# Sixteen words allocated in front of the weights of a directional convolution

## The reference

```python
x = x + _L0_conv_ref(_gn(x), L0_conv_dw_weight, L0_conv_pw_weight, L0_conv_pw_bias)
# in _L0_conv_ref:
h = gelu(depthwise3x3(x))                              # 256 channels
maps = einsum('bchw,oc->bohw', h, pw_weight) + pw_bias # 8 x 256 channels
for i, (dx, dy) in enumerate(OFFSETS8):
    diff = roll(x, (dy, dx)) - x
    out = out + maps[:, i] * diff
```

## Time and profile before

| | before |
|---|---|
| median of 3 runs | 2271.36 us |
| profiled execution | 2271.6 us |
| its span | 2269.8 us |
| granted TensorE clock, mean | 0.999 |
| TensorE busy | 97% |
| VectorE busy | 91% |
| GpSimd busy | 87% |
| ScalarE busy | 81% |

### The profile page before, as it was taken

The page is one execution under the profiler, slowest core; times in us unless marked ns, Lnnn a source line. Parts: engine busy times, 40 slices in busy tenths (PEclk is TensorE's granted clock), DMA queues, the critical chain, the costliest instruction groups (busy, mean ns, idle before and its releaser), DMA issues.

```text
span 2269.8 us, 28684 instructions
## 1 busy us (share of the span) xinstructions
PE 2209.1 (97%) x10752; PEld 2008.5 (88%) x10752; DVE 2056.1 (91%) x2234; ACT 1844.6 (81%) x2762; POOL 1981.4 (87%) x857
## 2 busy tenths in 40 slices
PE   1999999999999999999999999999999999999998
PEld 1999989999999999999989999999999999899997
DVE  7998989999999998998989999998999999999995
ACT  5978888788887978888788887888878888797774
POOL 5889898899888998899898988899888998889985
PEclk9999999999999999999999999999999999999999
DMA  6245263443725436164452644427353371542414
GB/s 179 51 82 116 49 115 88 90 98 56 156 41 106 95 54 153 33 108 95 77 127 39 116 98 84 103 49 136 68 98 90 64 156 33 106 98 49 98 33 73
DMA packets 47083, 202.13 MB, mean 89 GB/s; under 512 B 3040, under 2 KB 7136, under 8 KB 45664
## 3 DMA queue, kind: packets, MB, share of 16 engines
q0 software_dynamic: 30192, 94.97, 25.7%
q1 hardware_dynamic: 16752, 105.34, 18.0%
HBM read 104.88 MB, written 146.80 MB: 111 GB/s over the span
## 4 chain that ended last, share of the span: by engine, by line
PE 88%; DVE 5%; ACT 4%; issue 2%; DMA 0%; POOL 0%; SPq 0%; ACTq 0%; DVEq 0%
PE psum L913 88%; ACT psum L590 1%; DVE psum L705 1%; ACT hid L575 1%; DVE psum L785 1%; ACT psum L561 1%; DVE acc L727 1%; DVE products L705 1%; DVE psum L776 1%; DMA acc<-x 0%; ACT psum L565 0%; DVE acc L757 0%; POOL hlo L338 0%; DVE fields L808 0%; DVE part_sums L795 0%
## 5 line engine op out<-in xcount | busy, mean ns | idle before, releaser
L590 ACT ACTIVATE psum<-psum,bias,rstd 128x448 f32<-128x448 f32 x1792 | 1205.9, 694 | 384.6 <-PE psum L913 381.9
L369 POOL TENSOR_TENSOR acc<-acc,products 128x896 f32<-128x896 f32 x333 | 1167.1, 3505 | 240.2 <-DVE products L705 232.5
L913 PE MATMUL psum<-hhi,w_hi 128*128 128x448 f32 x3584 | 1321.7, 369 | 53.9 <-ACT hhi L580 45.5
L913 PE MATMUL psum<-hhi,w_lo 128*128 128x448 f32 x3584 | 1312.3, 366 | 0.0
L913 PE MATMUL psum<-hlo,w_hi 128*128 128x448 f32 x3584 | 1022.1, 366 | 0.3 <-POOL hlo L338 0.3
L785 DVE SCALAR_TENSOR_TENSOR psum<-xn,dw_f,psum 128x896 f32<-128x896 f32 x768 | 883.1, 1150 | 83.0 <-ACT psum L565 79.5
L913 PEld LDWEIGHTS psum<-hhi,w_hi 128*128 128x128 f32 x3584 | 672.6, 188 | 137.1 <-issue 45.5
L913 PEld LDWEIGHTS psum<-hlo,w_hi 128*128 128x128 f32 x3584 | 672.3, 188 | 59.7 <-POOL hlo L338 0.9
L913 PEld LDWEIGHTS psum<-hhi,w_lo 128*128 128x128 f32 x3584 | 672.8, 188 | 57.6
L705 DVE TENSOR_TENSOR products<-psum,fields 128x896 f32<-128x896 f32 x555 | 603.3, 1087 | 38.8 <-ACT psum L590 38.8
L705 DVE TENSOR_TENSOR acc<-psum,fields 128x896 f32<-128x896 f32 x224 | 242.6, 1090 | 53.2 <-ACT psum L590 51.8
(11 more groups left out here) (67 smaller groups left out, 449.0 us busy)
## 6 DMA issues: line engine op xcount, KB each, us to landing
out<-acc POOLq DMA_DIRECT2D x96, 896.0 KB, 7.7
out<-x SPq DMA_DIRECT2D x16, 3136.0 KB, 12.6
xpad<-x SPq DMA_DIRECT2D x30, 1568.0 KB, 15.1
out<-acc POOLq DMA_DIRECT2D x15, 448.0 KB, 5.6
acc<-x SPq DMA_DIRECT2D x4, 784.0 KB, 6.9
xpad<-pw_t SPq DMA_DIRECT2D x1, 2048.0 KB, 12.2
out<-products SPq DMA_DIRECT2D x2, 224.0 KB, 1.9
dw_f<-dw SPq DMA_DIRECT2D x1, 9.0 KB, 8.1
```

Source lines behind the costliest of these rows:

```text
L369: nc.gpsimd.tensor_tensor(a, a, p, ALU.add).then_inc(added_s, 1)
L590: nc.scalar.activation(m, m, ACT.Identity, bias=bias[ip][:, g, d:d + 1], scale=rstd[ip][:, g:g + 1]).then_inc(biased_s, 1)
L913: last = nc.tensor.matmul(maps(q)[:, side, :], w[:, kk, col:col + P], h_part(h, t, nl, kk), start=s == 0, stop=s == len(steps) - 1)
```

## The change

One tensor of sixteen float32 words a partition is allocated between `fields` and `w_hi`. Nothing reads or writes it.

```diff
@@ -111,6 +111,8 @@
         first = sums_t[:, 0:HALVES * H * W]
         first = first.rearrange("p (g c r w) -> p g c r w", g=HALVES, c=SLICES, w=W)
         w_raw = xpad_t[1][:, 0:HALVES * DIRS * C].rearrange("p (k m) -> p k m", k=HALVES)
+
+        sb("gap", [P, 16])
         w_hi = sb("w_hi", [P, HALVES, DIRS * C], F32R)
         w_lo = sb("w_lo", [P, HALVES, DIRS * C], F32R)
         dw_f = sb("dw_f", [P, HALVES, 9])
```

## The result

The changed kernel takes 2255.61 us in the median of six runs (2250.48 to 2258.2), against 2271.46 us before (2271.27 to 2272.06). The ratio is 0.9929, with a 95% interval of 0.9918 to 0.9939: 0.7% faster, where I had forecast no change. The scatter is new too: 7.7 us between the runs of one kernel, against 0.8 before.

What follows compares the result with a forecast made beforehand. PE was taken as the bound, by 10752 matmuls times their spacing. The sum 2269.8 + 0 + 0 + 0, and 1.8 outside, gave 2271.6 us profiled and 2271.4 for the median; range 2262 to 2281.

Steps and rivals of the forecast that it cites:

- The bound: On PE, time is nearly 10752 matmuls times their 203.75 ns spacing; each nanosecond of spacing is 10.75 us.
- What can tell the two starts apart: Weight starts at 32 and 96 of 128 bytes: only a structure of 128 bytes or more can distinguish them.
- The count of 128-byte blocks (five and five): A 512-byte weight read touches five 128-byte blocks from either start; the first gives 8 columns in place of 24.
- The load's cover: On PE, each weight load has at least 0.08 us of cover before its own matmul.
- the term for the loads: Effect of the moved weights on PE's weight loads: 10752 x 0 ns = 0.
- The 16.25 ns between the spacing and the stream: PE's 203.75 ns spacing less the 187.5 ns pure stream; if due to the weights' place, 175 us less.
- +12.5: Upper bound per matmul without cover: first block 16 columns shorter, 12.5 ns, 134 us more in all.
- a wrong handover term: On PE, the handover term would be wrong if loads stay at 188 ns and the spacing moves.
- The nearest row: VectorE's products reading windows at many starts average 1087 and 1090 ns, 0.3% apart; 0.5 ns of a load, hidden under cover.
- The one-off and the moved scalars: Writing the weights once: 0, under 12 us of cover; moved scalars on VectorE and ScalarE: 0, with 1 us of room.
- The faster rival: New start saves a step per load or handover: 0.8 ns, 8.6 us, 2262.8; whole excess about 2120; chance 0.10.
- The range: Whole kernel: 2262 to 2281 us, taking in one 0.8 ns step of spacing on either side.

Runs made afterwards that it cites:

- behind16: Sixteen words allocated behind both weight tensors instead of in front, against the kernel before the change: 2271.72 us, ratio 0.9998.
- either scan: Two kernels with only weight loads and matmuls, in bursts of 48, at various starts of weights and moving operand; spacings measured, no kernel time given.
- 96/0: Stage of a kernel of only loads and matmuls, ten bursts, weights from byte 96 of 128, moving operand at byte 0: 200.0 and 206.7 ns a matmul.

## Why the prediction was wrong

- **The bound.** Right: the spacing is the lever, 10.75 us a nanosecond. It moved by 2.08 ns, and the span's change is that less the longer waits.
- **What can tell the two starts apart.** Right that nothing that repeats every 64 bytes can. The count of 128-byte blocks (five and five) said nothing: the period is 256 bytes and it is the difference to `hhi` and `hlo` that counts, which I never worked out. It was 32 and became 96.
- **The load's cover.** Right as far as it went: trains with loads of 108 ns have no shorter spacing than trains with loads of 188. But cover of the load's length doesn't make the load free of effect: the same stream had 200.0 ns with loads of 128 columns and 206.7 with loads of 32.
- **"So the term for the loads is 10752 x 0 ns = 0."** This is the step that failed. From "the load is hidden" I went to "the weights' place costs nothing". The 16.25 ns between the spacing and the stream stood beside the sum as a lower bound (17.3 by the starts in ns: 203.96 less half of the 373.3 at half clock), and I set it aside since no row tied it to the weights. No row could: in the trace of before every load had the same difference. What the runs show in place of 0 is -2.08 ns a matmul, 22.3 us, between bounds of -16.25 and +12.5. The sign that the prediction had named for a wrong handover term came: the loads stayed at 188 ns and the spacing moved.
- **The nearest row.** VectorE's windows at many starts were the wrong neighbour. That engine's 0.3% says nothing on a pair of operands that PE reads side by side. The nearer sign was in the records themselves: two locked values, 203.3 and 204.4, taken by whole stretches between waits. The mean of 203.75 that I took from sixteen steps hid them.
- **The one-off and the moved scalars.** Right: `behind16` is the kernel of before, to 0.12%, and after the change PE starts at 45.4 us as before (45.5).
- **The faster rival.** It named the place, not a reason, with one column's step of 0.8 ns and 0.10. The direction was its own, but the step was 2.08 ns, and no run ties it to a column of the load. The Trainium skill ("TensorE: Matmul & The Clock Gate", "Back-to-back issue gap") gives 189.2 ns as the gap of an isolated matmul of 448 columns, and says that in a stream with loads both instructions set the spacing; the prediction left out that condition. No difference in either scan came under 200.0 ns with 448 columns, and the measurement decides.
- **The range.** 2262 to 2281 left out 2255.6. It had been drawn at one step of 0.8 ns on either side, with no row that said a step is that size.

## What to carry to other kernels

Where PE is the bound and each matmul has its own load, read the spacing of the starts in single nanoseconds, by stretches between waits, and compare it with columns over clock. If it is longer, try the start of the stationary operand against the moving one at a few differences modulo 256; a burst kernel with nothing but loads and matmuls gives the table in one run, and the kernel followed it at all six differences tried here (32, 64, 96, 128, 160 and 192). The table has to be taken with the kernel's own column counts: with 512 moving or 96 stationary columns the order of the differences was another. Then look at the waits, since a faster train gives part of its gain to them.

## What the runs showed of the hardware that I had not expected

With 448 moving columns and 128 stationary ones in float32r at a granted clock of 1.0, a train of loads and matmuls locks into one of a few mean spacings between 200.0 and 206.7 ns. Which ones are open depends on the difference of the two operands' starts modulo 256 bytes. Which of them is taken seems to depend on the moment at which the train starts after a wait: 96/0 had 200.0 in seven bursts and 206.7 in three, and the kernel changes nothing between them but the length of ScalarE's read, hence of the wait. The means are near whole parts between two ends: 200.0 and 206.7 are 30 and 31 times 6.67 ns, the time of sixteen moving columns (448 of them take 373.3 ns at half clock, so 186.7 at full clock); 203.3 is their half, 202.2 and 204.4 their thirds, 205.3 four fifths. The 173.3 ns of 384 columns and the 233.3 of 512 are 26 and 35 times 6.67 as well. That points to two readers that meet on a grid, but this was only argued from the numbers. What the grid is, and why 192 bytes is the best of the sixteen differences at these column counts, stays open. At 1.2 GHz the steps of the kernel before were 373 or 374 ns, which is 448 columns at that clock (373.3), with nothing above it.
